# The embedded-value matmuls of the relative attentions: weights of 32 columns on four column strips in place of 64 on two

## The chip, the cores and the metric

The kernel runs on one core of one Trainium2 chip. The metric is the device time of one execution in microseconds (us), median over several executions. Engines are named as the profile names them: PE is the matmul engine (TensorE), PEld its weight loads, DVE VectorE, ACT ScalarE, POOL GpSimd, SP SyncE.

## What is computed

The network passes a residual stream of 4 sequences of 512 tokens with 128 features through eight blocks: a four-layer transformer with local and linear attention, a mixture of experts, a relative attention with a causal mask, the mixture of experts again, a second relative attention without mask, a two-layer windowed transformer, a long-convolution block, and the windowed transformer again. The change touches the two relative attentions. Each has 16 heads of 8 features. The first one is, cut to what matters (x has batch B = 4, T = 512):

```python
rel = jnp.tril(idx[:, None] - idx[None, :]); rk = embk[rel]; rv = embv[rel]
att = jnp.einsum('bhtd,bhsd->bhts', q, k) * scale + jnp.einsum('bhtd,tsd->bhts', q, rk)
att = jax.nn.softmax(jnp.where(causal, att, -jnp.inf), axis=-1)
y = jnp.einsum('bhts,bhsd->bhtd', att, v) + jnp.einsum('bhts,tsd->bhtd', att, rv)
```

The second has the same form with distances clipped to -128 to 128 and no mask. The last term, the attention weights times the values that are looked up by distance (`rv`), is the "embedded values" of this case: to each pair of query and key belongs a row of 8 features that depends on their distance alone.

## The kernel before, in words

All work is fp32, in one program with an instruction stream written for each engine, tied by semaphores. A plan (`make_plan`) lays the stages out one after another; each relative attention is one step of it, `core`, with `which` 0 for the first and 1 for the second. The 2048 queries of a `core` are cut into 256 tiles of 8 queries times 16 heads, so 128 rows each (`Tile`); 16 tiles are one batch, which is one block of 128 queries of one sequence (`lane`); a lane has 4 blocks. The first attention needs `nk` = block + 1 blocks of keys, the second always 4.

The order on every engine is written out by hand: `core_steps` counts T_ up by two, and in each step every function handles the tiles T_ - lag and T_ - lag + 1. On PE a step is (lines 1048 to 1058):

- `scores` of two tiles: query times keys and distance table into `bank[0]` and `bank[1]`, then `spread` every second step (into `bank[6]`);
- `turn` of two tiles (line 984): the weights of the softmax transposed, block by block, into `bank[2]` and `bank[3]`; ACT copies them to `PT` (`turned`, line 1217);
- `embedded` of two tiles: the function that is changed. For each block of 128 keys near the query (two blocks in the first attention; two or three in the second: three where the query's block is 1 or 2) one matmul, with 64 columns of weights (8 queries times 8 features of the table, 128 keys deep) and `PT` of that tile as the moving operand, 128 columns read in runs of 8. The output goes to `bank[4]` or `bank[5]`: the first block's to partitions 0 to 63, the second's to 64 to 127, the third's again to 0 to 63, added. Where the block before the first does not exist, the weights are 64 columns of zeros;
- `values` in four of each eight steps: VS as weights of 32 columns on four column strips, into `bank[7]`. A step does two of a batch's eight parts: 4 matmuls for each block of keys, so 4 to 16 matmuls in the first attention and 16 in the second. Only the first part of a batch waits for semaphores;
- `fold`: 16 matmuls with 64 moving columns, weights of 32 columns on four strips. It adds up what DVE has picked from the embedded values (`chosen`, line 1625, into `WB`). It comes twice in a batch, from the lags FOLDS: in the first attention both times in a step that has `values`; in the second once with `values` and once alone behind `embedded`.

So `embedded` is followed on PE by `values`, by `fold` alone, or by the next step's `scores`. A matmul in fp32 shows in the profile as two weight loads and two matmul records; such a record is called a pass here. All plain matmuls are recorded under the helper `mm`, line 766.

On DVE a step is: `chosen` of two tiles, copies of folded parts (`position_copy`, lines 1653 and 1658, second attention only), `maxima` of the two tiles of scores (line 1640), `normal` (lines 1617 and 1618), `diagonal` (line 1633) every second step, `normal`. `diagonal` fills `B4`, for which the fourth scores matmul of the next step waits.

Of the kernel before, what the change touches and what calls it, by code (L numbers as in the profile page):

```python
# [22 lines left out]
P = 128  # L23
# [12 lines left out]
HEADS_R, D_R, QG = 16, 8, 8  # L36
# [410 lines left out]
def hybrid_network(nc, ins, scratch, out):  # L447
    plan, released, bank_of, tile_before = make_plan()
    ctx = ExitStack()
    with ctx:  # L450
# [5 lines left out]
        def sem(name):  # L456
            if name not in sems:
                sems[name] = ctx.enter_context(nc.semaphore(name))
            return sems[name]
# [28 lines left out]
        def carve(*shape):  # L488

            size = 1  # L490
            for s in shape:
                size *= s
            a = place[0][:, cursor[0]:cursor[0] + size]
            cursor[0] += size
            assert cursor[0] <= place[1], cursor[0]
            if len(shape) == 1:
                return a
            names = "abcd"[:len(shape)]
            return a.rearrange(f"p ({' '.join(names)}) -> p {' '.join(names)}",
                               **{n: s for n, s in zip(names[1:], shape[1:])})  # L500
# [38 lines left out]
        PT = carve(3, NT, HEADS_R, QG * QG)  # L539
# [47 lines left out]
        def k_(name):  # L587
            a, w = CONST[name]
            return const[:, a:a + w]
# [34 lines left out]
        def reached(eng, name, count):  # L624

            if not isinstance(count, int) or count > 0:
                eng.wait_ge(sem(name), count)
# [129 lines left out]
        def _(pe):  # L757
# [7 lines left out]
            def mm(o, l, r, start=True, stop=True):  # L765
                return pe.matmul(o, l, r, start=start, stop=stop)  # L766
# [156 lines left out]
            def core(s):  # L923
# [63 lines left out]
                def embedded(t):  # L987
                    pe.wait_ge(sem("r_turn_copied"), t.at + 1)
                    reached(pe, "r_chosen", t.at - 1)
                    o = bank[4 + t.G % 2]  # L990
                    if s.which == 0:
                        blocks = [t.block - 1, t.block]
                    else:
                        blocks = [b for b in (t.block - 1, t.block, t.block + 1) if 0 <= b < NT]
                    for j, b in enumerate(blocks):
                        apart, first = b - t.block + 1, (P - QG - QG * t.g) * D_R
                        if b < 0:
                            rows_ = k_("zeros")
                        elif s.which and t.block < 2:
                            rows_ = near_right[apart][:, first:first + QG * D_R]  # L1000
                        else:
                            rows_ = value_table[:, P * D_R * apart + first:P * D_R * apart + first + QG * D_R]
                        strip = slice(64 * (j % 2), 64 * (j % 2) + 64)
                        last = mm(o[strip, 0:P], rows_, PT[:, t.slot, max(b, 0), :, t.cols], start=(j < 2), stop=(j + 2 >= len(blocks)))
                    last.then_inc(sem("r_embedded"), 1)

                def values(T_):
# [40 lines left out]
                for T_, st in core_steps(s.which):  # L1048
                    st(scores, SCORES)
                    st(scores, SCORES - 1)  # L1050
                    st(spread, SCORES - 2)
                    st(turn, TURN)
                    st(turn, TURN - 1)
                    st(embedded, EMBED)
                    st(embedded, EMBED - 1)
                    values(T_)
                    values(T_ + 1)
                    fold(T_)
# [979 lines left out]
```

## Time and profile before

| | |
|---|---|
| three runs | 3199.95 us median (3192.93 to 3224.83) |
| the profiled execution | 3195.13 us, its span 3193.4 us |
| mean granted PE clock over the span | 0.96 of full speed |
| busy share of the span | PE 91%, DVE 61%, ACT 59%, POOL 30% |

The profile is of the one execution in the second row; durations and starts in the sections below are from it. In a timeline row the first number is the start in us from the span's start, the second how long the merged instructions took together; matmuls overlap, so what a group costs PE is read from one start to the next start.

### The profile page before, as it was taken

Reading aid. Unit: us, or ns where it says so; the run is one execution under the profiler, and the core shown is the slowest. Engines: PE = TensorE matmul, PEld = TensorE weight load, DVE = VectorE, ACT = ScalarE, POOL = GpSimd, SP = SyncE. Lnnn points to the kernel's source line nnn. Section 1 sums busy time; section 2 is a strip of 40 time slices with the busy share of each in tenths; the row PEclk is TensorE's granted clock in tenths of the full one; section 3 lists DMA queues with packets and bytes.
Section 4 is the critical chain, followed back from the end, with each engine's and each line's share of the span. In section 5 each row is a group of like instructions: output and inputs, shape, how many; then the busy total and the mean of one; then the engine's idle time right before and its main releaser. Section 6 shows DMA issues by size and latency. Waiting matters only on the chain.

```text
span 3193.4 us, 58985 instructions
## 1 busy us (share of the span) xinstructions
PE 2899.5 (91%) x21844; PEld 2005.5 (63%) x21844; DVE 1939.9 (61%) x5736; ACT 1879.3 (59%) x4388; POOL 959.0 (30%) x812
## 2 busy tenths in 40 slices
PE   8999999987999999789999999887898898988987
PEld 6667676744888887458888887344355463544544
DVE  5444444445777776677878887664565325654653
ACT  5464646432666666056777776675676514765764
POOL 1000000011232331054555553443343113442441
PEclk9999999987899999799999999999999999999999
DMA  1010000000000000100000000310111002111110
GB/s 50 1 39 1 12 1 9 1 4 8 1 2 2 2 2 2 49 22 2 2 2 2 2 2 2 120 44 17 43 44 28 21 1 57 44 27 27 47 34 14
DMA packets 35263, 62.85 MB, mean 20 GB/s; under 512 B 11526, under 2 KB 15654, under 8 KB 33830
## 3 DMA queue, kind: packets, MB, share of 16 engines
q1 hardware_dynamic: 34982, 59.07, 6.7%
q8 instruction: 180, 2.95, 0.4%
q14 instruction: 101, 0.83, 0.1%
HBM read 23.48 MB, written 1.15 MB: 8 GB/s over the span
## 4 chain that ended last, share of the span: by engine, by line
PE 75%; DVE 9%; POOL 5%; ACT 5%; issue 4%; SPq 2%; DMA 1%; DVEq 0%; POOLq 0%; ACTq 0%
PE bank L766 65%; PE bank L984 5%; POOL work L1869 3%; PE bank L1099 3%; SPq L732 2%; PE bank L836 1%; ACT work L1217 1%; DVE work L1583 1%; DVE work L1727 1%; ACT bank L1225 1%; ACT squared L1227 1%; DVE work L1710 1%; DMA work<-work 1%; DVE work L1704 1%; DVE centered L1458 1%
## 5 line engine op out<-in xcount | busy, mean ns | idle before, releaser
L766 PEld LDWEIGHTS bank<-work 128*64 128x64 f32 (+3 forms) x4992 | 423.6, 166 | 180.9 <-issue 141.8
L766 PE MATMUL bank<-work 128*64 128x128 f32 (+8 forms) x4992 | 520.9, 294 | 7.3 <-ACT work L1217 6.8
L1302 ACT ACTIVATE low<-bank,low 128x512 f32<-128x512 f32 (+23 forms) x384 | 227.4, 593 | 339.4 <-DVE low L1640 335.6
L1217 ACT ACTIVATE low<-bank 128x512 f32<-128x512 f32 (+3 forms) x512 | 425.4, 941 | 1.7 <-PE bank L984 1.7
L766 PE MATMUL bank<-table_keys,halves 128*128 128x512 f32 (+3 forms) x1536 | 422.3, 384 | 0.7 <-ACT low L1302 0.6
L1640 DVE TENSOR_REDUCE low<-bank 128x1 f32<-128x512 f32 (+22 forms) x512 | 288.7, 571 | 167.6 <-PE bank L766 162.3
L1217 ACT ACTIVATE work<-bank 128x512 f32<-128x512 f32 (+5 forms) x469 | 250.9, 545 | 185.4 <-PE bank L766 84.2
L1830 POOL TENSOR_TENSOR halves<-squared,const 128x512 fp32r<-128x512 f32 x128 | 135.4, 1058 | 570.9 <-PE bank L766 570.9
L1788 POOL TENSOR_SCALAR normed<-normed,slot 128x512 f32<-128x512 f32 x48 | 75.4, 1571 | 711.6 <-DVE normed L1465 711.3
L766 PEld LDWEIGHTS bank<-table_keys,halves 128*128 128x128 f32 x1536 | 248.8, 194 | 56.6 <-issue 33.2
L1869 POOL TENSOR_TENSOR work<-work 128x768 f32<-128x768 f32 x128 | 187.7, 1466 | 218.1 <-DVE work L1731 216.2
L1338 ACT ACTIVATE work<-work 128x192 f32<-128x192 f32 (+1 forms) x512 | 218.7, 430 | 45.2 <-DVE work L1720 45.2
L1099 PE MATMUL bank<-const,work 128*128 128x128 f32 x896 | 134.0, 293 | 119.2 <-POOL work L1869 118.7
L766 PE MATMUL bank<-work,slot 128*128 128x512 f32 x408 | 197.7, 619 | 35.3 <-ACT work L1217 29.1
L1099 PEld LDWEIGHTS bank<-const,work 128*128 128x128 f32 x896 | 106.5, 149 | 194.6 <-POOL work L1869 180.2
L1618 DVE TENSOR_SCALAR low<-low 128x512 f32<-128x512 f32 (+23 forms) x384 | 206.4, 538 | 13.5
L766 PE MATMUL bank<-halves 128*128 128x128 f32 (+27 forms) x1024 | 207.5, 285 | 3.3 <-DVE halves L1633 3.3
L1720 DVE CUSTOM_DVE_ANT_0 work<-bank,const 128x192 f32<-128x192 f32 (+1 forms) x512 | 143.6, 336 | 109.6 <-PE bank L766 109.0
L1221 ACT ACTIVATE squared<-centered 128x512 f32<-128x512 f32 x80 | 50.1, 630 | 270.6 <-DVE centered L1458 270.4
L766 PEld LDWEIGHTS bank<-halves 128*128 128x128 f32 x1024 | 185.8, 194 | 37.4 <-DVE halves L1633 10.5
L766 PE MATMUL bank<-normed,slot 128*128 128x512 f32 x440 | 205.8, 611 | 1.7 <-POOL normed L1788 1.7
L1874 POOL TENSOR_TENSOR work<-work 128x512 f32<-128x512 f32 x128 | 162.8, 1272 | 131.4 <-DMA work<-work 120.3
(195 smaller groups left out, 5723.6 us busy)
## 6 DMA issues: line engine op xcount, KB each, us to landing
work<-work SPq DMA_DIRECT2D x512, 64.0 KB, 2.0
slot<-in_wW SPq DMA_DIRECT2D x4, 1605.5 KB, 6.8
slot<-in_wA SPq DMA_DIRECT2D x4, 837.0 KB, 6.1
table_low<-embv_padded SPq DMA_DIRECT2D x2, 1536.0 KB, 6.3
table<-in_dft SPq DMA_DIRECT2D x1, 3072.0 KB, 12.5
slot<-in_wE SPq DMA_DIRECT2D x2, 584.0 KB, 3.7
const<-in_const SPq DMA_DIRECT2D x1, 1094.0 KB, 5.2
squared<-in_x SPq DMA_DIRECT2D x4, 256.0 KB, 6.2
```

Of the source, the lines that this page charges most:

```text
L766: return pe.matmul(o, l, r, start=start, stop=stop)
L984: last = pe.transpose(o[:, b * P:(b + 1) * P], PR[t.G % 4][:, b * P:(b + 1) * P], ident)
L1099: last = pe.transpose(o[:, (2 * a + blk) * P:(2 * a + blk + 1) * P], PW[:, s.n % 3, 2 * u + a, blk * P:(blk + 1) * P], ident)
L1217: return act.activation(dst, src, ACT.Identity)
L1302: act.activation(PR[t.G % 4][:, 0:n], bank[t.G % 2][:, 0:n], ACT.Exp, bias=NBR[:, t.G % 4:t.G % 4 + 1], accum_out=RSR[:, t.G % 8:t.G % 8 + ...
L1338: last = act.activation(row, row, ACT.Exp, scale=-1.0, bias=small[:, one:one + 1], accum_out=small[:, 4 + one:5 + one])
L1618: dve.tensor_scalar(row, row, inverse, None, ALU.mult).then_inc(sem("r_normal"), 1)
L1640: dve.tensor_reduce(out=NBR[:, t.G % 4:t.G % 4 + 1], in_=bank[t.G % 2][:, 0:score_columns(t)], axis=AX.X, op=ALU.max, negate=True).then_in ...
L1720: dve.tensor_tensor_reduce(out=PW[:, s.n % 3, one, lo:256], in0=banks[a][:, 256 * u + lo:256 * u + 256], in1=k_("window_mask")[:, lo - 64: ...
L1830: pool.tensor_tensor(A4[:, half, Q % 2, :].rearrange("p (t h) -> p t h", h=HEADS_R), bc(one_lane.unsqueeze(2), [P, 4 * QG, HEADS_R]), bc(k ...
L1869: pool.tensor_tensor(row, row, bc(small_w[:, s.n % 4, 8:12].unsqueeze(2), [P, 4, 192]), ALU.mult).then_inc(sem("w_weighed"), 1)
L1874: pool.tensor_tensor(R1[:, s.n % 3, :], R1[:, s.n % 3, :], R2[:, s.n % 3, :], ALU.add).then_inc(sem("w_added"), 1)
```

## The change

Each embedded matmul of 64 weight columns becomes two of 32 columns, over the same moving operand. Of the first block the halves go to partitions 0 and 32, of the second to 64 and 96, of the third to 0 and 32. What is computed, the accumulation over blocks, the place of every result, the semaphores and the order of blocks stay.

```diff
-                        strip = slice(64 * (j % 2), 64 * (j % 2) + 64)
-                        last = mm(o[strip, 0:P], rows_, PT[:, t.slot, max(b, 0), :, t.cols], start=(j < 2), stop=(j + 2 >= len(blocks)))
+                        for part in range(0, QG * D_R, 32):
+                            to = 64 * (j % 2) + part
+                            last = mm(o[to:to + 32, 0:P], rows_[:, part:part + 32], PT[:, t.slot, max(b, 0), :, t.cols],
+                                      start=(j < 2), stop=(j + 2 >= len(blocks)))
                     last.then_inc(sem("r_embedded"), 1)
```

## Rows read from the trace of the kernel before

**Rows 1.** The page: busy time by engine, and the granted clock in 40 slices.
```profile
PE 2899.5 (91%) x21844; PEld 2005.5 (63%) x21844; DVE 1939.9 (61%) x5736; ACT 1879.3 (59%) x4388; POOL 959.0 (30%) x812
...
PEclk9999999987899999799999999999999999999999
```
**Rows 2.** Windows over the two relative attentions: start:end length, then busy us.
```profile
780.00:1262.00 482.00, 479.65 (x5527) 406.44 (x5530) 347.83 (x1107) 305.98 (x768) 137.97 (x136) 0.96 0.01 2
1430.00:1996.00 566.00, 561.51 (x6491) 465.10 (x6484) 458.69 (x1185) 405.66 (x712) 283.17 (x240) 1.00 0.01 2
```
**Rows 3.** The chain by line, 930 to 1030 us and 1500 to 1600 us.
```profile
by line: PE bank L766 83.4%; PE bank L984 16.7%
...
by line: PE bank L766 73.2%; PE bank L984 16.6%; ACT low L1302 2.4%; DVE low L1640 2.1%; DVE low L1618 1.3%; DVE halves L1633 1.2%; DVE low L1653 0.9%; issue 0.9%; DVE low L1617 0.5%; DVE centered L1658 0.5%; DVE slot L1625 0.5%
```
**Rows 4.** PE's timeline, 943 to 945 us: `embedded`, `values`, next scores.
```profile
944.06 0.66 PE L766 MATMUL bank<-low,table_low 128*64 128x128 f32 x8
944.64 0.43 PE L766 MATMUL bank<-low 128*32 128x128 f32 x8
945.00 0.51 PE L766 MATMUL bank<-table_keys,halves 128*128 128x256 f32 x2
```
**Rows 5.** PE's timeline, 1595 to 1597 us: `values` of 32 passes, next scores.
```profile
1595.42 1.08 PE L766 MATMUL bank<-low 128*32 128x128 f32 x32
1596.43 0.50 PE L766 MATMUL bank<-table_keys,halves 128*128 128x512 f32 x1
```
**Rows 6.** PE's timeline, 1643 to 1646 us: `embedded` of three blocks, `fold`, next scores.
```profile
1643.89 1.09 PE L766 MATMUL bank<-low,table_low 128*64 128x128 f32 x12
1644.91 0.65 PE L766 MATMUL bank<-slot,const 128*32 128x64 f32 x32
1645.50 0.96 PE L766 MATMUL bank<-table_keys,halves 128*128 128x512 f32 x3
```
**Rows 7.** PE's timeline, 994 to 996 us: `values` of 24 passes, `fold`, next scores.
```profile
994.47 0.86 PE L766 MATMUL bank<-low 128*32 128x128 f32 x24
995.15 0.63 PE L766 MATMUL bank<-slot,const 128*32 128x64 f32 x32
995.71 0.73 PE L766 MATMUL bank<-table_keys,halves 128*128 128x512 f32 x2
```
**Rows 8.** The weight loads of that same place, with PEld's idle time before them.
```profile
994.47 0.59 PEld L766 LDWEIGHTS bank<-low 128*32 128x32 f32 x24 [0.17 <-issue]
995.04 0.57 PEld L766 LDWEIGHTS bank<-slot,const 128*32 128x32 f32 x32
```
**Rows 9.** Weight loads by form, 780 to 1996 us: xcount, busy us, mean ns, idle before.
```profile
L766 PEld LDWEIGHTS bank<-low,table_low 128*64 128x64 f32 x1792 | 124.2, 137 | 27.6 <-issue 27.4
L766 PEld LDWEIGHTS bank<-low 128*32 128x32 f32 x3328 | 83.3, 109 | 20.9 <-issue 20.9
```
**Rows 10.** Waits of 1430 to 1996 us, of PE's weight loads: total, times, longest.
```profile
PEld bank L766 <- DVE halves L1633: 6.3, 14, 0.7
```
**Rows 11.** DVE's and PE's timelines, 1644 to 1651 us.
```profile
1645.27 0.48 DVE L1625 TENSOR_TENSOR slot<-bank,const 128x128 f32<-128x128 f32 x2
...
1647.30 1.29 DVE L1640 TENSOR_REDUCE low<-bank 128x1 f32<-128x512 f32 x2
...
1650.02 0.68 DVE L1633 TENSOR_TENSOR halves<-bank,const 128x512 fp32r<-128x512 f32 x1
...
1646.29 0.41 PE L766 MATMUL bank<-halves 128*128 128x272 f32 x2
...
1650.75 0.51 PE L766 MATMUL bank<-halves 128*128 128x256 f32 x2
```
**Rows 12.** PE's timeline, 798 us: the first tiles' `embedded`, zeros as the first block.
```profile
798.30 0.48 PE L766 MATMUL bank<-low,const 128*64 128x128 f32 x1
798.31 0.48 PE L766 MATMUL bank<-low,table_low 128*64 128x128 f32 x1
798.57 0.42 PE L766 MATMUL bank<-low,const 128*64 128x128 f32 x1
798.58 0.42 PE L766 MATMUL bank<-low,table_low 128*64 128x128 f32 x1
```

## The prediction

> **What bounds the kernel now.** I read the page first. PE is busy 91% of the span and nothing else is above 61%, so any change to PE's instruction stream can reach the end [rows 1]. The windows over the two stretches where the changed function runs say more: in the first relative attention PE is busy 479.65 of 482 us, DVE 347.83, ACT 305.98; in the second 561.51 of 566, DVE 458.69 (81%) and ACT 405.66 (72%) [rows 2]. The chain of work agrees: in 100 us of the first attention it is PE alone; in 100 us of the second PE has 90%, and the rest is ACT L1302 and several lines of DVE [rows 3]. So the question is how long PE needs from the first `embedded` pass to the first pass of what comes next, and in the second attention whether DVE lets PE keep what it gains.
>
> **How a strip stretch is priced.** Passes on different strips run beside each other, so what counts is passes per strip. `values` of 8 passes, 2 per strip, took 945.00 - 944.64 = 0.36 us to the next start [rows 4]; of 32 passes, 8 per strip, 1596.43 - 1595.42 = 1.01 [rows 5]. The difference is 0.65 us for 6 more passes on each strip, 0.108 to 0.11 us a pass; I use 0.109. Taken off, both leave 0.14 us that does not depend on the count. `embedded` with 64 columns and two blocks (8 passes of two tiles, 4 per strip) took 944.64 - 944.06 = 0.58 [rows 4]: 4 x 0.109 + 0.15. With three blocks (12 passes, 8 of them on strip 0) it took 1644.91 - 1643.89 = 1.02 [rows 6]: 8 x 0.109 + 0.15. So a 64-column pass costs its strip what a 32-column pass costs, and every stretch pays about 0.15 us once.
>
> What is that 0.15? Between `values` and `fold`, which both use 32 columns on four strips, it is not there. `values` of 24 passes starts at 994.47, `fold` at 995.15, the next scores at 995.71 [rows 7]: 0.68 us for 6 passes per strip (0.65) leaves 0.03; `fold` in 0.56, where its 8 passes per strip with half the moving columns cost 8 x 0.055 = 0.44, leaves 0.12. Together 0.15 for both. The weight loads show the same: PEld sits idle 0.17 us before the loads of `values`, which follow those with 64 columns, and not at all before those of `fold` [rows 8]. Over both attentions this idle time is 20.9 us ahead of the loads of `values` [rows 9], about 120 times 0.17, which is how often `values` follows `embedded`. So the 0.15 us belongs to the change of strip width, and `embedded` with 32 columns shares one with whatever follows at 32 columns.
>
> **What the change adds.** 1152 matmuls (256 tiles x 2 blocks, and 64 tiles for each of 10 blocks over the four query blocks of the second attention) become 2304, so 2304 more weight loads and 2304 more passes. On the strips: with two blocks each tile had 2 passes on each of two strips, now it has 2 on each of four. With three blocks it had 4 on strip 0 and 2 on strip 1, now 4 on each of strips 0 and 1 and 2 on 2 and 3. The busiest strip has as many passes as before, so the streaming term is 0. Weight loads: a load of 32 columns shows 109 ns, of 64 columns 137 [rows 9], and in `values` four strips take 32 loads without delaying the 0.109 a pass; so the loads cost 0 as well, hidden by the passes. What comes with them is stepping over four strips instead of two at the end of a stretch, some 0.01 us, against a start that is some 0.025 us shorter (0.14 against 0.15 above): a stretch that stands alone gains 0.014. No semaphore, DMA or wait is added; DVE's `chosen` still waits for the last pass.
>
> **The sum.** `embedded` runs 128 times as a pair of tiles in each attention.
> - First attention: 61 pairs are followed by `values` (four steps of each batch, less the last three, when no tile is left). The two stretches become one, with one 0.15 less: 61 x 0.15 = 9.2 us. The other 67 gain 0.014: 0.9 us. Sum 10.1.
> - Second attention: 61 followed by `values` and 16 by `fold` alone [rows 6], again 0.15 each, whether with two blocks or three: 77 x 0.15 = 11.6 us. The other 51: 0.7. Sum 12.3.
>
> That is 22.4 us if PE bounds throughout. What is late next is DVE. PE waits for L1633 14 times in the second attention, 6.3 us together [rows 10]. One such place: DVE is late from L1625 at 1645.27 on: its two reduces run one behind the other from 1647.30, though the first tile's scores ended at 1646.70, and L1633 ends at 1650.70; PE's pass that waits for it begins at 1650.75 [rows 11]. The `fold` at 1644.91 [rows 6] stands just ahead of this stretch, so what PE gains there it only waits longer. It is the lone `fold` of each of 16 batches: 16 x 0.15 = 2.4 us lost, and about 0.4 of the small gains near it. In the steps with `values` DVE has room: over the whole second attention it idles 107 of 566 us [rows 2], and the gain asked of it there is 9. Net 22.4 - 2.8 = 19.6 us. From the profiled execution's 3195.1 us (span 3193.4 and 1.7 around it) this gives 3175.5. The median shown, 3199.95, lies 4.8 above that execution, but the lowest run lies 2.2 below, and I stay with the execution: **3176 us**.
>
> **Bounds of what is not shown.** No row has four strips reading the same short runs (8 elements) as moving operand; `embedded` does it on two, `values` does runs of 64 on four. Nearest row below: 0.109 a pass, nothing added. Above: if four strips shared what two get now, a pass would take 0.218. I take 0.109, since both neighbours have it. The seam itself lies between 0 and 0.17 us; I take 0.15, as between `values` and `fold`. The part that DVE eats lies between 0 and the second attention's whole 12.3.
>
> **A rule against this change.** The rows at 798 us show strip 0 (zeros) and strip 1 (table). The code issues the whole matmul of strip 0 first, both passes. Yet strip 1's first pass begins at 798.31, 0.01 behind strip 0's, and strip 0's second only at 798.57 [rows 12]. So passes of different strips do not wait for program order. The Trainium skill, page "TensorE: Matmul & The Clock Gate", section "Part 3: Packing small matmuls", says that matmuls start and end strictly in program order. By that rule the two passes of each 32-column matmul would hold the next strip back; the time that this gives is in rival 3. The rows of this case disagree with it.
>
> **Rivals.**
> 1. DVE takes back all of the second attention's gain: its busy share of 81% and the 10% of the chain outside PE speak for it; that `values` steps have no PE wait speaks against. 3195.1 - 10.1 = 3185.
> 2. The change doesn't do what it says: the 0.15 us comes not from the width but from the start of another function's stretch. Then only 256 x 0.014 = 3.6 us are gained: 3191.5. Against it: the missing idle before `fold` [rows 8].
> 3. Slower: the four strips don't run beside each other for this operand. If every 32-column matmul holds the next strip for its 0.109 + 0.007, a pair costs 8 x 0.116 + 0.14 = 1.07 in place of 0.59 (192 pairs) and 12 x 0.116 + 0.14 = 1.53 in place of 1.02 (64): 92 + 33 = 125 us, less the 22 at the seams: 3195.1 + 103 = 3298. A pass that is slowed by sharing decides the sign from 0.126 us on: the busiest strips have 192 x 4 + 64 x 8 = 1280 passes, and 22 / 1280 = 0.017. Against it: `values` has the same order of strips and passes, and its 16 matmuls took 1.01 us, not 16 x 0.116 = 1.86 [rows 5].
>
> **How the numbers follow.** Forecast (3171 to 3181) 0.74, rival 1 0.12, rival 2 0.07, rival 3 0.06, other 0.01. Runs of the same kernel spread from 3193 to 3225, so a median may lie some us off. The range goes from 3166 (all 22.4 us, and a low median) to 3196 (rival 2 and a high one). A measurement of this kernel can tell about 1%, 32 us, from no change. No case gives 32 us of gain, which leaves 0.06 for noise; slower by over 1% is rival 3, 0.05; the rest, 0.89, is within 1%.
>
> **What would show it.** Right: `embedded` as 16 and 24 passes of 128*32; 0.58 us alone; next to `values` no PEld idle before the loads of `values`, and from the first pass of `embedded` to the scores behind 8 passes of `values` 0.79 us in place of 0.94; idle "issue" of 20.9 us near 0; the first attention shorter by 10 us, the second by 9, and PE's wait for L1633 up from 6.3 to about 8.5. Wrong: a pair of tiles that takes over 0.6 us alone, or the 0.17 still there.

## The result and the profile after

The changed kernel takes 3179.55 us (median of 14 runs, 3169.02 to 3198.00) against 3204.82 us (14 runs, 3192.93 to 3224.83). The ratio is 0.9922, 95% interval 0.9898 to 0.9946: faster by 0.8%, between 17 and 33 us. The forecast was 3176 us and 19.6 us of gain. The profiled execution took 3175.59 us with a span of 3173.8.

The page of the changed kernel answers [rows 1]: 2304 more passes and 2304 more weight loads, and less busy time on PE all the same.

```profile
PE 2879.0 (91%) x24148; PEld 2005.6 (63%) x24148; DVE 1938.1 (61%) x5736; ACT 1879.3 (59%) x4388; POOL 959.5 (30%) x812
...
PEclk9999999988999999899999999998999999999998
```

PE's timeline of the changed kernel has the places that the prediction priced. First a pair of tiles with two blocks and `values` of 8 passes, which answers [rows 4]; then `values` and `fold` behind it, which answers [rows 7]; then three blocks with the lone `fold`, which answers [rows 6]; last, three blocks alone.

```profile
935.02 0.65 PE L766 MATMUL bank<-low,table_low 128*32 128x128 f32 x16
935.48 0.40 PE L766 MATMUL bank<-low 128*32 128x128 f32 x8
935.81 0.62 PE L766 MATMUL bank<-table_keys,halves 128*128 128x256 f32 x3
...
983.88 0.65 PE L766 MATMUL bank<-low,table_low 128*32 128x128 f32 x16
984.34 0.84 PE L766 MATMUL bank<-low 128*32 128x128 f32 x24
985.00 0.63 PE L766 MATMUL bank<-slot,const 128*32 128x64 f32 x32
985.56 0.72 PE L766 MATMUL bank<-table_keys,halves 128*128 128x512 f32 x2
...
1623.05 0.96 PE L766 MATMUL bank<-low,table_low 128*32 128x128 f32 x22
1623.74 0.31 PE L766 MATMUL bank<-slot,const 128*32 128x64 f32 x4
1623.84 0.28 PE L766 MATMUL bank<-low,table_low 128*32 128x128 f32 x2
1623.95 0.62 PE L766 MATMUL bank<-slot,const 128*32 128x64 f32 x28
1624.49 0.73 PE L766 MATMUL bank<-table_keys,halves 128*128 128x512 f32 x2
...
1579.92 0.42 PE L766 MATMUL bank<-low,shifted 128*32 128x128 f32 x8
...
1580.92 0.96 PE L766 MATMUL bank<-table_keys,halves 128*128 128x512 f32 x3
```

What to see: from the first pass of `embedded` to the scores it is 935.81 - 935.02 = 0.79 us where it was 0.94, as forecast. With `values` of 24 passes and a `fold` it is 1.68 us, which is 10 x 0.109 + 8 x 0.055 + 0.15: one fixed cost for three functions. Three blocks with the lone `fold` take 1.44 us where they took 1.61. Three blocks alone take 1.00 where they took 1.02, and two blocks alone 0.57 (946.80 to 947.37), where the prediction's sign of being wrong was over 0.60. The third group also shows four passes of `fold` starting before the last two of `embedded`. By the program these last two stand on strips 0 and 1, and `fold`'s four can only be those of strips 2 and 3, where `embedded` has fewer passes; the rows do not name the strip.

Pass by pass, the two middle lanes of the second attention show the price of one change of width in both kernels: 0.203 us from the start of the last pass of one width to the start of the first of the next, at every change (128 to 64, 64 to 32, 32 to 128 columns), where passes of one width follow each other by 0.109 us.

The weight loads of the second place answer [rows 8], and those of both attentions [rows 9]; the loads by form have the columns xcount, busy us, mean ns, idle before.

```profile
983.88 0.38 PEld L766 LDWEIGHTS bank<-low,table_low 128*32 128x32 f32 x16 [0.17 <-issue]
984.23 0.68 PEld L766 LDWEIGHTS bank<-low 128*32 128x32 f32 x24
984.89 0.58 PEld L766 LDWEIGHTS bank<-slot,const 128*32 128x32 f32 x32
...
L766 PEld LDWEIGHTS bank<-low,table_low 128*32 128x32 f32 x3584 | 111.9, 109 | 27.7 <-issue 27.5
L766 PEld LDWEIGHTS bank<-low 128*32 128x32 f32 x3328 | 96.3, 110 | 0.4 <-issue 0.4
```

The idle 0.17 us stays ahead of `embedded`, where the full array gives way to strips (27.4 us before, 27.5 after), and is gone ahead of `values`: 20.9 us before, 0.4 after.

To see how much of this arrives, I read the length of a lane (64 tiles, 32 steps) from the starts of DVE's L1640 (L1642 in the changed file, and so two more for each line behind the change), from a lane's first reduce to the next lane's. The windows below lie on these starts. Kernel before: up to the first attention, its first lane, its second lane, the whole second attention, the rest.

```profile
0.00:780.62 780.62, 697.15 (x3666) 481.96 (x3666) 387.84 (x1308) 395.36 (x946) 68.31 (x47) 0.94 0.04 13
780.62:906.15 125.53, 125.53 (x1195) 106.58 (x1195) 86.33 (x272) 74.55 (x190) 34.37 (x32) 0.86 0.01 2
906.15:1023.18 117.03, 116.80 (x1410) 98.96 (x1410) 87.01 (x278) 76.39 (x193) 36.02 (x36) 1.00 0.01 2
1391.44:1984.62 593.18, 590.13 (x6585) 488.22 (x6584) 487.29 (x1251) 431.61 (x760) 309.41 (x262) 1.00 0.01 2
1984.62:3193.00 1208.38, 1036.86 (x5693) 575.16 (x5692) 640.67 (x1870) 724.54 (x1877) 431.37 (x355) 0.96 0.14 38
```

The same stretches of the changed kernel:

```profile
0.00:783.25 783.25, 699.72 (x3666) 483.89 (x3666) 388.12 (x1309) 395.62 (x946) 68.30 (x47) 0.93 0.04 13
783.25:898.03 114.78, 114.70 (x1435) 98.46 (x1435) 85.77 (x273) 74.45 (x190) 34.43 (x32) 0.93 0.01 2
898.03:1012.56 114.53, 114.26 (x1666) 98.70 (x1666) 86.93 (x278) 76.51 (x193) 36.09 (x36) 1.00 0.01 2
1374.21:1956.85 582.64, 578.61 (x7845) 487.85 (x7848) 486.75 (x1251) 431.41 (x760) 309.78 (x262) 1.00 0.01 2
1956.85:3173.00 1216.15, 1043.95 (x5716) 582.80 (x5714) 639.86 (x1870) 724.33 (x1877) 431.26 (x355) 0.95 0.14 37
```

At full clock a lane of the first attention went from 117.03 to 114.53 us (its second lane). A lane of the second went from 150.00 (1538.08 to 1688.08) to 146.95 us (1519.38 to 1666.32). Four times these are 10.0 and 12.2 us. A full-clock lane has 16 places where `values` follows, four lanes 64, but an attention has 61; without three of them the change is worth 9.6 and 11.8 us, together 21.4. Taken directly, the second attention from its first reduce to its last fell by less, from 593.18 to 582.64 us. It lost 1.1 us ahead of its third reduce, before any changed matmul had run: the first tensor_scalar of `normal` took 2.05 us there (at 1376.41), beside POOL, where it took 0.53 in the kernel before. With the 1.1 us and the one seam behind the last reduce it is 11.8 us again. The first attention's first lane fell by 10.7 us, over 8 more than the change explains, because in this execution less of it ran at the lower clock (0.86 against 0.93 granted). The stretch ahead of the attentions, which the change does not touch, was 2.6 us longer, and the one behind the last reduce 7.8, both at a lower granted clock. So the span's 19.6 us agrees with the forecast to the digit by chance; the lanes are the measurement to hold against the steps.

### The profile page after: what moved, and what is told of

It is laid out like the page before. It is cut to its first block, busy times and chain, and to the rows that moved or that the text cites. A ratio compares the mean times of both kernels' runs of the same rounds, so it can differ in the third digit from the quotient of the medians.

```text
span 3173.8 us, 63593 instructions
## 1 busy us (share of the span) xinstructions
PE 2879.0 (91%) x24148; PEld 2005.6 (63%) x24148; DVE 1938.1 (61%) x5736; ACT 1879.3 (59%) x4388; POOL 959.5 (30%) x812
## 4 chain that ended last, share of the span: by engine, by line
PE 75%; DVE 9%; ACT 5%; POOL 4%; issue 4%; SPq 2%; DMA 1%; DVEq 0%; POOLq 0%; ACTq 0%
PE bank L766 64%; PE bank L984 5%; PE bank L1101 3%; POOL work L1871 3%; SPq L732 2%; PE bank L836 1%; ACT work L1219 1%; DVE work L1585 1%; ACT bank L1227 1%; ACT squared L1229 1%; DVE work L1729 1%; DVE work L1712 1%; DVE work L1706 1%; DVE centered L1460 1%; DMA work<-work 1%
## 5 line engine op out<-in xcount | busy, mean ns | idle before, releaser
L766 PEld LDWEIGHTS bank<-work 128*64 128x64 f32 (+3 forms) x4992 | 432.3, 169 | 182.0 <-issue 140.6
L766 PE MATMUL bank<-work 128*64 128x128 f32 (+8 forms) x4992 | 531.4, 299 | 7.3 <-ACT work L1219 6.8
L1642 DVE TENSOR_REDUCE low<-bank 128x1 f32<-128x512 f32 (+22 forms) x512 | 288.3, 571 | 144.2 <-PE bank L766 140.6
```

What stands on the lines that cost most here:

```text
L1642: dve.tensor_reduce(out=NBR[:, t.G % 4:t.G % 4 + 1], in_=bank[t.G % 2][:, 0:score_columns(t)], axis=AX.X, op=ALU.max, negate=True).then_in ...
```

## The experiments

Each table row is one profiled execution; its lanes are at full clock (the second lane of each attention). The time beside it is the median of 14 runs for the changed kernel, of 4 for balanced, of 6 for balanced_pool and balanced_first, and one run for the others; the last column is the kernel before on the same chip (14 or 11 runs, but one for the 3203.98).

| kernel | lane of the first attention, us | lane of the second, us | time, us | before, us |
|---|---|---|---|---|
| before | 117.03 | 150.00 | | |
| changed | 114.53 | 146.95 | 3179.55 | 3204.82 |
| apart64 | 118.65 | 152.63 | 3239.28 | 3203.98 |
| apart32 | 118.27 | 152.15 | 3222.85 | 3203.98 |
| alone32 | 116.87 | 149.91 | 3199.23 | 3203.98 |
| diag_first | 114.46 | 150.61 | 3207.01 | 3203.98 |
| pool_later | 113.71 | 150.31 | 3185.33 | 3210.28 |
| pool_short_b | 116.20 | 149.62 | 3210.08 | 3203.90 |
| pool_short | 113.71 | 146.70 | 3168.28 | 3203.90 |
| balanced | 114.49 | 144.07 | 3172.72 | 3210.28 |
| balanced_pool | 113.67 | 148.88 | 3185.53 | 3210.28 |
| balanced_first | 113.67 | 144.08 | 3173.80 | 3203.90 |

### Is it the seam or the width? apart64, apart32, alone32

Two kernels move `embedded` away from `values`; they differ from each other as the kernel before and the changed one do:

```diff
+                    st(embedded, EMBED)
+                    st(embedded, EMBED - 1)
                     st(turn, TURN)
                     st(turn, TURN - 1)
-                    st(embedded, EMBED)
-                    st(embedded, EMBED - 1)
```

> The kernel before, with the 64-column embedded matmuls moved ahead of turn, so that they never stand next to values or fold. Theory (each change between full width, 64 and 32 columns is paid for once): a step with values or a lone fold has one more change and one more refill of full-width weights, some 0.2 us: a lane of the first attention goes from 117.0 us to about 120.2, of the second from 150.0 to about 154. This kernel is the partner of apart32.

> The changed kernel, with the 32-column embedded matmuls moved ahead of turn in the same way. Theory (the gain is the change of width that embedded and values share): with the shared place gone the gain goes too: a lane is only some 0.45 us shorter than in apart64 (32 pairs of tiles times 0.014 us), about 119.8 and 153.6 us. Rival (32 columns on four strips are cheaper in themselves): the lanes are shorter than apart64's by 2.5 us in the first attention and 3.1 in the second, as the changed kernel's are against the kernel before.

Between the two, a lane differs by 118.65 - 118.27 = 0.38 us and 152.63 - 152.15 = 0.48 us, where 0.45 was expected and the rival wanted 2.5 and 3.1. The rival that 32 columns are cheaper in themselves is out. Without the shared seam, 32 columns are worth 0.014 us a pair and no more. One number missed: apart64 is only 1.6 and 2.6 us a lane above the kernel before, not 3.2 and 4. An extra change of width costs about 0.1 us here (1.6 / 16, and 2.6 / 20 = 0.13), where I had put 0.2; 0.203 - 0.109 = 0.094 us of it stands between two passes. What apart32 lost against the changed kernel is 3.7 us in 16 places of the first attention, 0.23 us each: the 0.15 of the seam and this 0.1.

alone32 gives 32 columns only to the pairs that scores follow:

```diff
+                def alone(t):
+                    step = t.G // 2 * 2 + EMBED
+                    follows = step >= VALUES and (step - VALUES) % BATCH < QG
+                    return not (follows or (s.which and batch_after(step, FOLDS[1][0]) is not None))
...
-                        for part in range(0, QG * D_R, 32):
+                        width = 32 if alone(t) else 64
+                        for part in range(0, QG * D_R, width):
                             to = 64 * (j % 2) + part
-                            last = mm(o[to:to + 32, 0:P], rows_[:, part:part + 32], PT[:, t.slot, max(b, 0), :, t.cols],
+                            last = mm(o[to:to + width, 0:P], rows_[:, part:part + width], PT[:, t.slot, max(b, 0), :, t.cols],
```

> Only those embedded matmuls have 32 columns that are followed by scores; where values or fold follow, they keep 64. Theory (the gain is in the seam): a lane shrinks by 16 x 0.014 = 0.22 us in the first attention (117.03 to 116.8) and by 12 x 0.016 = 0.2 in the second (150.0 to 149.8). Rival (32 columns are cheaper wherever they stand): about half of the gain, 115.8 and 148.5 us.

The lanes fell by 0.16 and 0.09 us. So of the changed kernel's 2.50 and 3.05 us a lane, over 90% are in the pairs that `values` or `fold` follow: 2.34 / 16 = 0.146 us and 2.96 / 20 = 0.148 us for each, against 0.15 in the forecast.

### Why DVE did not take its share: diag_first, pool_later, pool_short

The prediction took off 2.8 us because PE waits for DVE's `diagonal` behind each lone `fold`. The waits of PE's weight loads over the whole second attention, kernel before and then changed kernel (total us, times, longest):

```profile
PEld bank L766 <- DVE halves L1633: 8.0, 16, 1.1
PEld bank L766 <- ACT low L1302: 3.3, 15, 0.7
```

```profile
PEld bank L766 <- DVE halves L1635: 8.1, 16, 1.1
PEld bank L766 <- ACT low L1304: 4.9, 19, 1.0
```

The waits for `diagonal` did not grow by the 2.2 us (6.3 to 8.5) that the prediction named. Those for ACT's exponentials grew by 1.6 us. The place of [rows 11] in the kernel before, DVE's and POOL's timelines:

```profile
1649.03 1.06 DVE L1618 TENSOR_SCALAR low<-low 128x512 f32<-128x512 f32 x1
1650.02 0.68 DVE L1633 TENSOR_TENSOR halves<-bank,const 128x512 fp32r<-128x512 f32 x1
...
1647.74 1.06 POOL L1830 TENSOR_TENSOR halves<-squared,const 128x512 fp32r<-128x512 f32 x1 [4.10 <-PE bank L766]
1648.75 1.06 POOL L1830 TENSOR_TENSOR halves<-inner,const 128x512 fp32r<-128x512 f32 x1
1649.77 1.47 POOL L1840 TENSOR_TENSOR halves<-squared,const 128x512 fp32r<-128x512 f32 x1
```

The same place of the changed kernel:

```profile
1626.45 1.29 DVE L1642 TENSOR_REDUCE low<-bank 128x1 f32<-128x512 f32 x2
...
1628.19 0.89 DVE L1620 TENSOR_SCALAR low<-low 128x512 f32<-128x512 f32 x1
1629.00 0.68 DVE L1635 TENSOR_TENSOR halves<-bank,const 128x512 fp32r<-128x512 f32 x1
...
1626.71 1.06 POOL L1832 TENSOR_TENSOR halves<-squared,const 128x512 fp32r<-128x512 f32 x1 [3.89 <-PE bank L766]
1627.73 1.06 POOL L1832 TENSOR_TENSOR halves<-inner,const 128x512 fp32r<-128x512 f32 x1
1628.75 1.47 POOL L1842 TENSOR_TENSOR halves<-squared,const 128x512 fp32r<-128x512 f32 x1
```

The tensor_scalar of `normal` takes 0.49 us where no POOL instruction stands beside it. Here it took 1.06 and 0.89, and in both kernels `diagonal` begins 0.25 us behind the start of POOL's third instruction (1650.02 - 1649.77, 1629.00 - 1628.75). POOL's first one had waited for PE's scores of that very step, which stand behind the `fold`. Counted from the first pass of `embedded` (1643.89 and 1623.05), DVE's two reduces start at 3.41 and 3.40 us and the tensor_scalar at 5.14 in both kernels, so DVE's own work did not move up. POOL's first instruction did, from 3.85 to 3.66, and `diagonal` with it, from 6.13 to 5.95. So what made `diagonal` late was tied to PE after the place of the gain, and moved up with it. The Trainium skill, page "SBUF — State Buffer", section "SBUF: two separate sides", says that a DVE instruction in a two-port performance mode and a GpSimd instruction take one shared pair of ports in turn, each for its whole length. The rows fit it: the tensor_scalar started inside POOL's second instruction and ended 0.28 us behind that one's end (1650.09 against 1649.81). That this tensor_scalar runs in such a mode is assumed; no run here shows the mode.

The first trial moved `diagonal` out of the way:

```diff
                     st(maxima, SCORES)
                     st(maxima, SCORES - 1)
+                    st(diagonal, SCORES - 2)
                     st(normal, SCORES)
-                    st(diagonal, SCORES - 2)
                     st(normal, SCORES - 1)
```

> The changed kernel, with diagonal put ahead of both normal on DVE. In the changed kernel PE still waits 6.3 us for diagonal in the second attention, and what diagonal stands behind there is a tensor_scalar of normal that takes 0.9 to 1.3 us instead of 0.49 and ends with a POOL instruction. Theory (diagonal is late because that one instruction waits for POOL, which itself started behind the scores of the same step): the waits for diagonal go, a lane of the second attention falls from 146.94 us by some 1.5 to 1.9 us, of the first from 114.54 by some 0.9. Rival (DVE is simply full between two places where it catches up): the lateness moves to the next instruction that PE needs, and the lanes stay within 0.3 us.

The waits for `diagonal` went, but a lane of the second attention grew by 3.7 us; the first attention gained 0.1. Waits of PE's weight loads and of its matmuls in diag_first, second attention:

```profile
PEld bank L766 <- ACT low L1304: 13.0, 26, 1.0
PEld bank L984 <- DVE slot L1620: 3.5, 11, 0.5
...
PE bank L766 <- ACT low L1304: 5.7, 14, 0.8
PE bank L766 <- DVE low L1655: 4.9, 7, 0.8
```

The lateness moved to the exponentials and to the copies of folded parts, and became larger. DVE never sat idle ahead of `diagonal` here, so it is not a wait for PE's `spread`. What grew is the tensor_scalars: the 64 of the second lane took 51.2 us together, 29 of them over 0.6 us each, where they took 38.7 us with 16 such in the changed kernel. The windows over that lane, of these instructions alone (start:end length, then DVE's busy time; diag_first, then the changed kernel):

```profile
1540.07:1690.68 150.61, 51.22 (x64) 1.00 0.01 2
1519.38:1666.32 146.94, 38.65 (x64) 1.00 0.01 2
```

The likely reason is that, with `diagonal` ahead of them, more of them run beside POOL. Neither the theory's number nor the rival's "within 0.3" came out. The second trial moved POOL instead:

```diff
-                        pool.wait_ge(sem("r_scores"), t.at - t.G % 4 - 4)
+                        pool.wait_ge(sem("r_normal"), t.at - t.G % 4 - 4)
```

> The changed kernel; POOL's spreading of the queries (L1832, L1842) waits for normal of the tiles in place of their scores, so it starts when DVE's tensor_scalar of that step is done; diagonal keeps its place. Theory (diagonal is late only because that tensor_scalar stands still until a POOL instruction ends): the tensor_scalar takes 0.49 us there as elsewhere, the waits for diagonal go, and a lane of the second attention falls from 146.94 us to 145.0 to 145.6. Rival (DVE is full, POOL has no part in it): the durations and the lanes stay.

The first attention gained 0.83 us a lane, the second lost 3.4. POOL has four of these instructions there (some 5 us in each 9), and started later they meet other tensor_scalars (47.9 us for the 64 of the second lane, the longest 1.60) and end late for PE's `spread`. The waits for `diagonal`, which were to go, grew, as those of PE's weight loads in pool_later show:

```profile
PEld bank L766 <- DVE halves L1635: 10.9, 24, 0.8
PEld bank L766 <- POOL halves L1842: 5.8, 7, 0.9
```

So POOL's phase matters by several us a lane, but this did not single out the one meeting. The third trial took three quarters of POOL's work away, in both kernels; each leaves out the scores of three tiles in four, so its result is no longer the network's:

```diff
                     queries = (QR_HI, QR_LO)[half]
+                    n = 4 * QG if t.G < 16 else QG
...
-                                           bc(one_lane.unsqueeze(2), [P, 4 * QG, HEADS_R]),
+                                           bc(one_lane.unsqueeze(2), [P, n, HEADS_R]),
```

(and so for the outputs, the inputs and `AX4`.)

> The kernel before, with POOL's spreading of the queries cut to a quarter from the second batch of each attention on (8 of 32 queries of a chunk; the rest of A4 and AX4 keeps old contents, so the scores of three tiles in four are left out of the computation). Theory (PE waits for diagonal only because DVE's tensor_scalar stands still behind a POOL instruction): the tensor_scalar takes 0.49 us everywhere, the waits for diagonal go, a lane of the second attention falls from 150.0 to about 148 us. Rival (DVE is full by itself): lanes and waits stay. This kernel is the partner of pool_short.

> The changed kernel with the same cut of POOL's work, and so with the same part left out. A lane of the second attention falls from 146.94 to about 145 us, and against pool_short_b the change is worth the same 3.07 us a lane as with POOL's full work, since in neither does DVE take any of it. If DVE had been taking part of the gain, the difference would grow here, to over 3.3.

In pool_short, the place from before:

```profile
1624.34 0.49 DVE L1620 TENSOR_SCALAR low<-low 128x512 f32<-128x512 f32 x1
1624.74 0.68 DVE L1635 TENSOR_TENSOR halves<-bank,const 128x512 fp32r<-128x512 f32 x1
...
1625.87 0.40 PE L766 MATMUL bank<-halves 128*128 128x256 f32 x2
```

The tensor_scalar takes 0.49 us, `diagonal` ends at 1625.42, and PE, which comes to it at 1625.87, no longer waits. That is the theory's picture, for the two middle blocks of each lane. In the first attention it holds throughout: no tensor_scalar of the second lane takes over 0.50 us, and the lane is 0.83 us shorter in both kernels. But the second attention's lanes fell by 0.4 (before) and 0.25 us (changed), not by 2: in the first and last block of a lane PE waits for `diagonal` with POOL short as well. Read batch by batch (16 tiles, by the same starts), the change is worth, in us:

| block of the lane | 0 | 1 | 2 | 3 |
|---|---|---|---|---|
| with POOL's full work | 0.72 | 0.79 | 0.80 | 0.73 |
| with POOL's short work | 0.63 | 0.81 | 0.82 | 0.64 |
| the sum of its seams and lone pairs | 0.79 | 0.79 | 0.79 | 0.79 |

With POOL short, blocks 0 and 3 lose about one seam of 0.15 us a batch, which is what the prediction took off for all; blocks 1 and 2 lose nothing. With POOL's full work the loss is 0.07 in blocks 0 and 3. What the changed kernel fails to keep is therefore about 2 x 0.07 us a lane, 0.5 us in all. Which engine takes it is not shown: in the second lane PE's waits for `diagonal` did not grow (1.90 us before, 1.89 after, of its weight loads), while those for ACT's exponentials went from 0.5 to 1.0. In the short kernels the waits for `diagonal` did grow, from 1.19 to 1.32 us. The difference between the short kernels, 2.92 us a lane, is smaller than the 3.05 between the full ones, so both of my lines for pool_short (3.07, or over 3.3) were wrong, in the direction that a little of the gain is lost to DVE when POOL's work is short.

### The strips of a pair with three blocks: balanced, balanced_pool, balanced_first

With three blocks, strips 0 and 1 have 8 passes for a pair of tiles and strips 2 and 3 have 4. The masks and the fold treat both halves of the partitions alike, so every second tile can be turned over:

```diff
-                            to = 64 * (j % 2) + part
+                            to = 64 * ((j + t.g) % 2) + part
```

> The changed kernel, with the two halves of the output swapped for every second tile: its first block goes to partitions 64 and 96, its second to 0 and 32. A pair of tiles with three blocks then has 6 passes on each of the four strips in place of 8 on two and 4 on the others. Theory (the busiest strip sets the length): 2 x 0.109 us less for each of the 16 such pairs of a lane of the second attention, 146.94 to 143.5 us, the first attention unchanged at 114.54; 14 us over the kernel, so about 1.2% under the kernel before. Rival (DVE and ACT hold the second attention by then): lanes of 145 to 146.5.

A pair alone in this kernel:

```profile
1590.75 0.43 PE L766 MATMUL bank<-low,shifted 128*32 128x128 f32 x8
...
1591.54 0.96 PE L766 MATMUL bank<-table_keys,halves 128*128 128x512 f32 x3
```

It takes 0.79 us where it took 1.00. A lane of the second attention takes 144.07 us, 2.9 less, of the 3.5 expected; of the rest, 0.4 us stands in PE's waits for `diagonal`, which rose from 1.89 to 2.32 us a lane. Against the kernel before the ratio is 0.9891 (0.9871 to 0.9911), 3172.72 us against 3210.28.

> Both edits, the balanced strips and POOL's later start. If POOL's instruction is what makes diagonal late, the two gains add: lanes of 141.5 to 142.5 us in the second attention and some 20 us in all under the changed kernel. If DVE is full, it is no better than balanced alone.

The two gains did not add, and it came out worse than the other line, "no better than balanced alone": 148.88 us, POOL's later start costs 4.8 us a lane on top of balanced. Ratio 0.9932 (0.9907 to 0.9957).

The last kernel keeps POOL's later start for the first attention:

```diff
-                        pool.wait_ge(sem("r_scores"), t.at - t.G % 4 - 4)
+                        pool.wait_ge(sem("r_scores" if s.which else "r_normal"), t.at - t.G % 4 - 4)
```

> The balanced strips, and POOL's later start in the first attention alone, where it gained 0.83 us a lane. The two should add: lanes of 113.7 us in the first attention and 144.1 in the second, 3.3 us under the balanced kernel, which is less than its interval.

Lanes of 113.67 and 144.08 us: the two add. The ratio to the kernel before is 0.9882 (0.9853 to 0.9911), 3173.80 us against 3203.90. By its lanes it is 3.4 + 11.5 = 15 us ahead of the changed kernel; by its times alone, the intervals of the two ratios still overlap.

## Why the prediction was right

- **What bounds it.** Right. PE was the bound in both attentions: a lane of the first fell by 2.50 us, where its 16 seams and 16 lone pairs come to 2.62.
- **The pass.** Right: 0.109 us a strip with four strips reading runs of 8, the point that no row had shown. Rival 3 is refuted by the lengths: 0.57 us for two blocks alone where it had 1.07. The rule that passes keep program order is refuted by the rows around 1623.74, where `fold` overtakes `embedded`.
- **The seam.** Right: 0.15 us forecast, 0.146 and 0.148 measured. Rival 2, that the cost belongs to the start of another function, fell with the result itself: `values` still follows `embedded`, and the idle time ahead of its loads went from 20.9 to 0.4 us. apart32 and alone32 exclude something else, that 32 columns are cheaper in themselves.
- **A stretch alone.** Right: 0.014 us a pair forecast; 0.16 / 16 = 0.010 and 0.09 / 12 = 0.008 in alone32, 0.012 and 0.015 between the apart kernels. Its working was weaker than its number: the prediction takes 0.025 us for the shorter start and points at 0.14 against 0.15, which is 0.01, and the 0.01 for stepping over four strips is an estimate that no row shows.
- **The sum.** First attention 10.1 forecast, 9.6 by its full-clock lane and its 61 seams. Second 12.3 before DVE's part, 11.8 by the same measure (10.5 between its first and last reduce, where 1.1 us was lost at its start). Counts and places were right; the seams were a little smaller than 0.15 us.
- **What DVE takes.** Mis-sized: 2.8 us forecast, at most about 0.5 measured. The step that failed is the reading of [rows 11] that DVE is late from L1625 on by its own work, and that what PE gains ahead of it is lost in waiting. DVE ran with one gap of 0.25 us, behind ACT, but the length of the stretch was no constant. One tensor_scalar in it was stretched by POOL, so that `diagonal` began 0.25 us behind the start of a POOL instruction, and POOL's start was tied to PE's scores behind the gain. The step holds as written only in blocks 0 and 3, and there in full only with POOL's short work.
- **The total.** 3176 forecast, 3179.55 measured, gain 19.6 forecast and 25.3 by the medians (17 to 33). The lanes' 21.4 us is inside. That the time came out 3.6 us from the forecast is in part luck. The forecast started from the profiled execution, 3195.1 us, which lies 9.7 below the median of 14 runs of the kernel before, and its gain was 5.7 us less than that of the medians; the two errors offset each other. That the profiled executions also differ by 19.6 us is luck as well: 21.4 us of the lanes, the 1.1 us at the start of the second attention, and differences of the clock. Such differences are large beside the gain: the stretch ahead of the attentions, the same in all kernels, took 780.6 to 799.9 us in the twelve profiled executions, at a granted clock of 0.94 to 0.92.

## What to carry to other kernels

A change of the strip width on PE cost 0.1 to 0.15 us each time in this kernel. Functions that follow each other on strips should use the same width, even if that doubles the number of matmuls; then count passes per strip and put the odd block on the emptier strips. Before a gain is written off to an engine that is late behind it, see whether that engine's stretch is made of its own work or is stretched by a third engine that is tied to PE further down.

## What the hardware showed beyond that

- The number of weight columns did not change a strip's time here: a pair with 16 passes of 32 columns took 0.57 us, with 8 of 64 columns 0.58.
- Strips run ahead of each other over the border of two functions, by up to four passes here.
- A DVE tensor_scalar from SBUF to SBUF, 128x512 fp32, took 0.49 us alone and up to four times that beside POOL's tensor_tensor instructions (2.05 us in the changed kernel at 1376.41; there POOL had one running without a gap from 1373.65 on).
- How long PE's clock stays low at the start of the first attention differs between executions: its first lane takes 6 to 9 us longer than the next in 7 of the 12 profiled executions (granted clock 0.86 or 0.87; 44 us at half clock in the kernel before, 24 in the changed one) and about as long in 5 (0.93 or 0.94). Both come with 32 and with 64 columns; with one execution a kernel, whether an edit has a part in it is not shown.
